# First slot of the expert projections: two token tiles per expert in turn, and all low halves of the weights on VectorE

## The chip, the cores and the metric

The kernel runs on one core of one Trainium2 chip. The metric is the device time of one execution in microseconds (us), as the median of several executions. The engines are TensorE (PE in the profile; PEld is its weight load), VectorE (DVE), ScalarE (ACT), GpSimd (POOL) and SyncE (SP), which issues most DMAs; ScalarE issues some too. Each engine works through its own list of instructions in order, and they meet through semaphores.

## What is computed

One block of a network on 4096 tokens of 256 channels: a normalised and modulated state space layer, and then an attention whose query, key, value and output projections are weighted sums over 16 experts. The part that matters here, cut from the reference:

```python
h = _layernorm(x) * (1 + ca) + sa
x = x + ga * attn_ref(h, ...)        # projection, short convolution, scan over tokens, gate, output projection
h = _layernorm(x) * (1 + cb) + sb
...
# n = 4096 tokens, c = 256, 16 experts, head size 128
logits = xn @ sn - sigmoid(gates)
w = softmax(masked relu(logits))     # at least two experts per token
def moe_proj(p):                     # p is q_proj, k_proj or v_proj: [16, 256, 128]
    y = einsum('nc,ech->neh', x, p)
    return einsum('ne,neh->nh', w, y)
q, k, v = moe_proj(q_proj), moe_proj(k_proj), moe_proj(v_proj)
attn = softmax(q k^T / sqrt(h))
out = sum over e of w[:, e] * (attn v) @ o_proj[e]
```

## The kernel before

The tokens are cut in 8 blocks of 512, each of 4 token tiles of 128. The first part of the kernel (to about 790 us) makes queries, keys and values, the second the attention. The first part is a row of 8 slots, one for each block: `slot(i, p, ahead)` for block 2i+p. A slot has 64 steps on TensorE, 4 tiles times 16 experts. **One step** is six matmuls (line 1793) that multiply one tile with one expert's query, key and value weights (384 columns) into one of four PSUM banks of `ps`: three for each half of the channels, since tokens and weights are kept as a high part and a low part (`xt_hi`, `xt_lo`, `w_hi`, `w_lo`). VectorE then adds the bank, times the token's weight for the expert, to `acc[:, t % 2]` (part of the memory `wst`; line 1478 for the first expert of a tile, line 1481 for the others), and counts `moe_acc`. TensorE may be three steps ahead of that (`wait(pe, moe_acc, ... s - MOE_BANKS + 1)`). Before, step s belongs to tile s // 16 and expert s % 16.

When a tile's 16 experts are summed, TensorE transposes its queries and keys into bank 7 (`qk_transposes`, lines 1698 and 1699), ScalarE rounds them and the values to high parts (`high_parts`, lines 842 and 845, counted by `v_hi_ready`), GpSimd makes the low part of the values (`low_v`, line 667, counted by `v_split`), VectorE that of queries and keys (`low_qk`, line 1264), and ScalarE issues the DMAs (`store_parts`). The first addition of tile t has to wait for `qk_mm` and `v_split` of tile t - 2, whose `acc` it writes over.

Between the steps stands the work of the next blocks, set by step numbers in a table (`DVE_PIECES`, `SCAN_AT`, `PE_Y`, ...). In the first slot they count from step 4 (`late`): r = s - 4. In the order of a slot these are, for block 1 (`c`): seven scan steps (TensorE line 1635, VectorE line 1112), `y_piece` at r = 24 (TensorE line 1652), the gate (VectorE line 1127), `out_piece` at r = 27 (TensorE line 1667), and `x2_piece` 0 at r = 29 (VectorE line 1140). For block 2 (`a`): `norm_piece` 0 to 4 on VectorE (lines 1023 and 1028, then 1039, 1046, 1023 and 1028, and 1033), in the first slot at the r of `LATE_NORMS`; `n2_transposes` at r = 20 (TensorE line 1563); `hidden` on ScalarE (lines 768 and 770 in turn), which counts `ht_ready`; and `project` from r = 31 (TensorE line 1579). Two waits matter. `y_piece` writes the banks that `hidden` reads and waits for it:

```python
if ahead >= 2 and not is_first(i, p):
    pe.wait_ge(ht_ready, upto(i, p, 1, 2))
```

And the first `project` of the slot waits for `x2_piece` 0, which reads those banks:

```python
if f == 0:
    pe.wait_ge(ht_lo_ready, upto(i, p, 1, 1))
    if i:
        pe.wait_ge(x2_ready, past(i, p, 1, 0, X2_MORE))
```

The low halves of the 16 experts' weights (`w_lo`) are made once, each by one subtraction of 128x768 elements. VectorE makes experts 0 to 7 ahead of the first slot and 8 to 10 in it (`split_w`, line 1018), GpSimd 11 to 15 (line 728), after `residual(0, 1)` (lines 628 and 632) and its part of `xt_lo` (line 723). In the first slot TensorE waits before each step of tile 0 for the expert's low half. VectorE makes the part of `xt_lo` that tile 0 needs (line 1456, `xlo_first`).

## Time and profile before

| what | us |
|---|---|
| median of 3 executions | 1403.19 |
| lowest and highest | 1401.58 and 1404.46 |
| the profiled execution | 1400.98 |
| its span | 1399.0 |
| TensorE busy in it | 1361.3 |
| VectorE, ScalarE, GpSimd busy in it | 1153.9, 685.4, 725.8 |

The span goes from the first to the last instruction of one execution. Some 2 us of the execution lie around it. Times of rows are counted from the span's start. The first slot's steps begin at 70.8 us. A row of an order of time has its start, its busy time, engine, line, operation, what is written and read, shapes and count; in brackets at its end stands how long the engine was idle before it and who ended that. A row can stand for several like instructions in a row, and its time is then from the first start to the last end.

### The profile page before, as it was taken

What the parts mean: (1) busy time and instruction counts of PE and PEld (TensorE: products, weight loads), DVE (VectorE), ACT (ScalarE), POOL (GpSimd) and SP (SyncE); (2) the same over time, 40 slices, a digit from 0 to 9 for tenths busy, and PEclk for the clock granted to TensorE, in tenths of its full rate; (3) what the DMA queues carried; (4) which work ended last, traced back from release to release, by engine and by line L of the source; (5) the groups of instructions that cost most, each with busy time, mean ns of one, the idle gap of its engine ahead of it and who ended that gap; (6) DMA issues with size and microseconds to landing.
All of it is one profiled execution on the core that took longest, in us unless ns stands there. A gap on an engine that the chain in (4) does not pass through costs nothing. (4 is left out here: it accounts for less than half of the span.)

```text
span 1399.0 us, 21090 instructions
## 1 busy us (share of the span) xinstructions
PE 1361.3 (97%) x6974; PEld 1204.5 (86%) x6974; DVE 1153.9 (82%) x2176; ACT 685.4 (49%) x1350; POOL 725.8 (52%) x641
## 2 busy tenths in 40 slices
PE   7989999999999999999999899999999999999997
PEld 5889999999999999999999777878787878788776
DVE  7886886868868778585778898989898989999866
ACT  4702314013121040320101598888888888888983
POOL 1551412214113140140123477888888888888897
PEclk9999999999999999999999999999999999999999
DMA  8201110111111101001147500000001010010000
GB/s 230 82 16 32 40 28 28 40 32 29 28 38 29 33 23 43 30 26 28 57 144 230 206 2 19 12 31 16 31 16 31 9 39 8 16 31 16 15 9 31
DMA packets 83389, 63.01 MB, mean 45 GB/s; under 512 B 14240, under 2 KB 76112, under 8 KB 83024
## 3 DMA queue, kind: packets, MB, share of 16 engines
q1 hardware_dynamic: 55136, 46.00, 10.5%
q10 hardware_dynamic: 28144, 15.67, 3.8%
q8 instruction: 55, 0.90, 0.3%
q14 instruction: 54, 0.44, 0.1%
HBM read 36.55 MB, written 25.03 MB: 44 GB/s over the span
## 5 line engine op out<-in xcount | busy, mean ns | idle before, releaser
L1793 PE MATMUL ps<-w_hi,memory_r 128*128 128x384 f32 x2048 | 561.2, 341 | 2.3 <-POOL w_lo L728 1.8
L1481 DVE SCALAR_TENSOR_TENSOR wst<-ps,w_cur,wst 128x384 f32<-128x384 f32 x480 | 295.2, 615 | 150.8 <-PE ps L1793 134.3
L2014 POOL TENSOR_TENSOR memory_rest<-memory_rest,pf 128x512 f32<-128x512 f32 x248 | 346.6, 1398 | 65.9 <-ACT pf L2121 57.2
L1793 PEld LDWEIGHTS ps<-w_hi,memory_r 128*128 128x128 f32 x2048 | 373.8, 188 | 6.9 <-issue 4.1
L1793 PE MATMUL ps<-w_lo,memory_r 128*128 128x384 f32 x1024 | 343.4, 335 | 0.0
L2187 DVE TENSOR_TENSOR p_lo<-pf,p_hi 128x512 fp32r<-128x512 f32 x256 | 281.8, 1101 | 33.1 <-ACT p_hi L2123 32.1
L1793 PEld LDWEIGHTS ps<-w_lo,memory_r 128*128 128x128 f32 x1024 | 192.6, 188 | 4.7 <-issue 1.4
L2121 ACT ACTIVATE pf<-ps 128x512 f32<-128x512 f32 x256 | 153.1, 598 | 72.3 <-PE ps L2293 54.3
L2081 ACT COPY ps<-shift_rows 128x512 f32<-128x512 f32 x254 | 151.7, 597 | 5.8
L2123 ACT ACTIVATE p_hi<-ps 128x512 fp32r<-128x512 f32 x256 | 152.0, 594 | 0.0
L2168 DVE TENSOR_REDUCE mx<-ps 128x1 f32<-128x512 f32 x224 | 147.7, 679 | 1.2 <-PE ps L2282 1.2
L667 POOL TENSOR_TENSOR wst<-wst 128x128 fp32r<-128x128 f32 x28 | 12.9, 461 | 239.8 <-ACT wst L845 239.8
L2204 DVE SCALAR_TENSOR_TENSOR memory_rest<-ps,w_out_s,memory_rest 128x256 f32<-128x256 f32 x252 | 120.7, 479 | 8.2 <-PE ps L2360 3.2
L1994 POOL TENSOR_TENSOR memory_rest<-memory_rest,act_half 128x256 f32<-128x256 f32 x112 | 108.1, 965 | 6.2 <-ACT act_half L2096 1.3
L2317 PE MATMUL ps<-p_hi,memory_kv 128*128 128x512 f32 x256 | 100.9, 394 | 7.4 <-DVE p_lo L2187 7.4
L2291 PE MATMUL ps<-memory_r 128*128 128x512 f32 x256 | 101.9, 398 | 5.5 <-ACT ps L2081 4.1
L842 ACT CAST wst<-ps 128x256 fp32r<-128x256 f32 x28 | 10.5, 373 | 194.5 <-PE ps L1699 194.1
L2360 PE MATMUL ps<-o_hi,ot_hi 128*128 128x512 f32 x256 | 100.0, 391 | 1.4 <-DVE ot_lo L2209 1.4
L2292 PE MATMUL ps<-memory_kv,memory_r 128*128 128x512 f32 x256 | 100.3, 392 | 0.0
L2293 PE MATMUL ps<-memory_r,memory_kv 128*128 128x512 f32 x256 | 100.3, 392 | 0.0
L2319 PE MATMUL ps<-p_lo,memory_kv 128*128 128x512 f32 x256 | 100.0, 391 | 0.0
L2318 PE MATMUL ps<-p_hi,v_lo 128*128 128x512 f32 x256 | 99.8, 390 | 0.0
(256 smaller groups left out, 2198.6 us busy)
## 6 DMA issues: line engine op xcount, KB each, us to landing
qk_scratch<-wst ACTq DMA_DIRECT2D x56, 128.0 KB, 2.2
x_scratch<-memory SPq DMA_DIRECT2D x8, 512.0 KB, 2.9
o_scratch<-memory_rest SPq DMA_DIRECT2D x16, 256.0 KB, 3.2
x2b<-x_scratch SPq DMA_DIRECT2D x32, 128.0 KB, 2.2
out_x<-memory_rest SPq DMA_DIRECT2D x32, 128.0 KB, 1.7
v_scratch<-wst ACTq DMA_DIRECT2D x60, 64.0 KB, 1.8
memory<-in_x SPq DMA_DIRECT2D x7, 512.0 KB, 4.1
memory_r<-qk_scratch SPq DMA_DIRECT2D x9, 256.0 KB, 4.4
```

Of the source, the lines that this page charges most:

```text
L1481: nc.vector.scalar_tensor_tensor(out=dst, in0=src, scalar=w, in1=dst, op0=ALU.mult, op1=ALU.add).then_inc(moe_acc, 1)
L1793: ins = nc.tensor.matmul(ps[:, s % MOE_BANKS, 0:H3], x_part[p][:, k, rows], w_part[:, k, e].rearrange("p t h -> p (t h)"), start=(k == 0 a ...
L1994: nc.gpsimd.tensor_tensor(total, total, halves[n], ALU.add).then_inc(act_summed, 1)
L2014: nc.gpsimd.tensor_tensor(p_sum[:, p], p_sum[:, p], pf[:, j % PB], ALU.add).then_inc(p_summed, 1)
L2081: nc.scalar.copy(ps[:, S_BANK + j % 2, :], shift_rows[:]).then_inc(seeded, 1)
L2121: nc.scalar.activation(pf[:, buf], ps[:, S_BANK + j % 2, :], ACT.Exp, scale=SCALE).then_inc(pf_ready, 1)
L2123: nc.scalar.activation(p_hi[:, buf], ps[:, S_BANK + j % 2, :], ACT.Exp, scale=SCALE).then_inc(p_hi_ready, 1)
L2168: nc.vector.tensor_reduce(mx[:, t, g:g + 1], ps[:, MAX_BANKS[j % 2], :], AX_X, ALU.max).then_inc(max_red, 1)
L2187: nc.vector.tensor_tensor(p_lo[:, j % PB], pf[:, j % PB], p_hi[:, j % PB].bitcast(F32), ALU.subtract).then_inc(p_lo_ready, 1)
L2204: nc.vector.scalar_tensor_tensor(out=y[:, t % 2], in0=src, scalar=w, in1=so_far, op0=ALU.mult, op1=ALU.add).then_inc(y_acc, 1)
L2291: nc.tensor.matmul(dst, k_hi[:, keys], q_hi[:, p], start=shifted, stop=False, skip_group_check=True)
L2317: nc.tensor.matmul(dst, v_hi[:, j], p_hi[:, buf], start=(j == 0), stop=False)
```

## The change

In the first slot alone, steps 0 to 31 take tiles 0 and 1 in turn for each expert: step s belongs to tile s % 2 and expert s // 2. VectorE makes the low halves of experts 0 to 5 ahead of the slot and those of 6 to 15 in it, one after each even step from step 6 to 24; GpSimd makes none. An addition then waits for the addition two steps back and not for the last one. Tile 0 is summed at step 30 and tile 1 at step 31, so the transposes of tile 0's queries and keys move from step 20 to step 33 and its `low_qk` from 22 to 35; tile 1's stay at 36 and 38. `LATE_NORMS` moves pieces 3 and 4 from r = 14 and 18 to 15 and 20, and `n2_transposes` moves from r = 20 to 23 in this slot; `y_piece` stays at r = 24. VectorE's first part of `xt_lo` grows from one tile to two. GpSimd's `residual(0, 1)` waits for the last `u_ready` of block 1 in place of the eighth low half. ScalarE and GpSimd take `hidden` and `low_hidden` of block 2 ahead of tile 0's parts.

```diff
-        LATE_SPLIT, POOL_SPLIT, SPLIT_AHEAD, FIRST_BU, FIRST_TAKE = 8, 11, 3, 3, 0
-        LATE_NORMS = {4: 0, 8: 1, 11: 2, 14: 3, 18: 4}
+        LATE_SPLIT, SPLIT_AHEAD, FIRST_BU, FIRST_TAKE, LATE_N2 = 6, 3, 3, 0, 3
+        LATE_NORMS = {4: 0, 8: 1, 11: 2, 15: 3, 20: 4}
...
+        def step(i, p, s):
+
+            if is_first(i, p) and s < 2 * E:
+                return s % 2, s // 2
+            return divmod(s, E)
+
+        def tile_sums(i, p, t):
+
+            return 2 * E - 1 + t if is_first(i, p) and t < 2 else (t + 1) * E
+
+        def tile_parts(i, p, s, at):
+
+            t, e = step(i, p, s)
+            if is_first(i, p) and s < 2 * E + at:
+                return 0 if s == 2 * E + at - 3 else None
+            return t - 1 if e == at and t else None
...
-                pool.wait_ge(w_lo_ready, LATE_SPLIT)
+                pool.wait_ge(u_ready, 2 * FI)
                 residual(0, 1)
-                rest = slice(P, BT)
+                rest = slice(2 * P, BT)
...
-                pool.wait_ge(w_lo_ready, POOL_SPLIT)
-                for n in range(POOL_SPLIT, E):
-                    pool.wait_ge(w_hi_ready, n + 1)
-                    nc.gpsimd.tensor_tensor(w_lo[:, :, n], w_raw[:, :, n], w_hi[:, :, n].bitcast(F32), ALU.subtract
-                                            ).then_inc(w_lo_ready, 1)
...
-                    if first:
-                        high(0)
                     if ahead >= 2:
                         hidden(*a)
-                    if not first:
-                        high(0)
+                    high(0)
                     store(0)
...
-                tt(xt_lo[0][:, :, 0:P], h2t[:, :, 0:P], xt_hi[0][:, :, 0:P].bitcast(F32), ALU.subtract
+                tt(xt_lo[0][:, :, 0:2 * P], h2t[:, :, 0:2 * P], xt_hi[0][:, :, 0:2 * P].bitcast(F32), ALU.subtract
...
-                split_w(6, LATE_SPLIT)
...
-                            dve.wait_ge(moe_acc, upto(i, p, STEPS, s))
+                            dve.wait_ge(moe_acc, upto(i, p, STEPS, s - 1 if is_first(i, p) and s < 2 * E else s))
...
-                        if is_first(i, p) and LATE_SPLIT <= s + SPLIT_AHEAD < POOL_SPLIT:
-                            split_w(s + SPLIT_AHEAD, s + SPLIT_AHEAD + 1)
+                        if is_first(i, p) and s % 2 == 0 and LATE_SPLIT <= s // 2 + SPLIT_AHEAD < E:
+                            split_w(s // 2 + SPLIT_AHEAD, s // 2 + SPLIT_AHEAD + 1)
...
-                            if r == PE_TRANSPOSE_N2:
+                            if r == PE_TRANSPOSE_N2 + (LATE_N2 if is_first(i, p) else 0):
                                 n2_transposes(*a)
```

TensorE from the transposes of block 2 (`ps<-ident,memory`) to `y_piece` (`ps<-st_parts,cm_parts`). Before, the transposes stand four steps of five rows each ahead of `y_piece`; these are the last step and `y_piece`:

```order
L1793 MATMUL ps<-w_hi,memory_r 128x384 [waits moe_acc]
L1793 MATMUL ps<-w_lo,memory_r 128x384
L1793 MATMUL ps<-w_hi,memory_r 128x384 x2
L1793 MATMUL ps<-w_lo,memory_r 128x384
L1793 MATMUL ps<-w_hi,memory_r 128x384
L1652 MATMUL ps<-st_parts,cm_parts 128x512 [waits ht_ready,st_in]
L1652 MATMUL ps<-st_parts,cm_parts 128x512 x2
```

The same place in the changed kernel (its line numbers are 11 to 15 higher there):

```order
L1574 MATMUL ps<-ident,memory 128x128 [waits n2_ready]
L1574 MATMUL ps<-ident,memory 128x128 x7
L1804 MATMUL ps<-w_hi,memory_r 128x384 [waits w_lo_ready,moe_acc]
L1804 MATMUL ps<-w_lo,memory_r 128x384
L1804 MATMUL ps<-w_hi,memory_r 128x384 x2
L1804 MATMUL ps<-w_lo,memory_r 128x384
L1804 MATMUL ps<-w_hi,memory_r 128x384
L1663 MATMUL ps<-st_parts,cm_parts 128x512 [waits ht_ready,st_in]
```

One step is left between the transposes and `y_piece`, where there were four.

ScalarE in the first slot, before: tile 0's parts (`wst<-ps`, `wst<-wst`), then `hidden` of block 2, then the stores:

```order
L842 CAST wst<-ps 128x256 [waits qk_mm]
L845 CAST wst<-wst 128x128
L768 ACTIVATE memory<-ps,lnb,lnw 128x512 [waits n2_transposed]
L770 ACTIVATE memory_r<-ps,lnb,lnw 128x512
L768 ACTIVATE memory<-ps,lnb,lnw 128x512
L770 ACTIVATE memory_r<-ps,lnb,lnw 128x512
L853 DMA qk_scratch<-wst 256x1x128 [waits qk_lo_ready,qk_ready]
```

And in the changed kernel:

```order
L783 ACTIVATE memory<-ps,lnb,lnw 128x512 [waits n2_transposed]
L785 ACTIVATE memory_r<-ps,lnb,lnw 128x512
L783 ACTIVATE memory<-ps,lnb,lnw 128x512
L785 ACTIVATE memory_r<-ps,lnb,lnw 128x512
L857 CAST wst<-ps 128x256 [waits qk_mm]
L860 CAST wst<-wst 128x128
L868 DMA qk_scratch<-wst 256x1x128 [waits qk_lo_ready,qk_ready]
```

`hidden` now comes first, and tile 0's parts stand directly ahead of its stores.

VectorE in the first slot, before, around the second part of the normalisation of block 2 (`memory<-memory,mv,modv`):

```order
L1481 SCALAR_TENSOR_TENSOR wst<-ps,w_cur,wst 128x384 [waits moe_acc,moe_mm] x2
L1112 TENSOR_TENSOR scan_b<-scan_b,ps 128x62 [waits scan_add,scan_mm]
L1481 SCALAR_TENSOR_TENSOR wst<-ps,w_cur,wst 128x384 [waits moe_acc,moe_mm] x2
L1112 TENSOR_TENSOR scan_b<-scan_b,ps 128x60 [waits scan_add,scan_mm]
L1039 SCALAR_TENSOR_TENSOR memory<-memory,mv,modv 128x256 [waits mv_ready,r_ready]
L1039 SCALAR_TENSOR_TENSOR memory<-memory,mv,modv 128x256 x3
```

And in the changed kernel:

```order
L1124 TENSOR_TENSOR scan_b<-scan_b,ps 128x62 [waits scan_add,scan_mm]
L1492 SCALAR_TENSOR_TENSOR wst<-ps,w_cur,wst 128x384 [waits moe_acc,moe_mm] x2
L1030 TENSOR_TENSOR w_lo<-w_raw,w_hi 128x2x384 [waits w_hi_ready]
L1124 TENSOR_TENSOR scan_b<-scan_b,ps 128x60 [waits scan_add,scan_mm]
L1051 SCALAR_TENSOR_TENSOR memory<-memory,mv,modv 128x256 [waits mv_ready,r_ready]
L1051 SCALAR_TENSOR_TENSOR memory<-memory,mv,modv 128x256 x3
L1492 SCALAR_TENSOR_TENSOR wst<-ps,w_cur,wst 128x384 [waits moe_acc,moe_mm] x2
L1030 TENSOR_TENSOR w_lo<-w_raw,w_hi 128x2x384 [waits w_hi_ready]
```

A low half stands after every second addition, ahead of the scan step that TensorE waits for.

## Rows read from the trace of the kernel before

**Rows 1.** The page's head, and the waits of TensorE, longest first, from 118 to 800 us

```profile
span 1399.0 us, 21090 instructions
...
PE ps L2291 <- ACT ps L2081: 1.4, 1, 1.4
```

**Rows 2.** Waits of TensorE from 70 to 135 us: us in total, times, longest

```profile
PE ps L1793 <- POOL w_lo L728: 1.8, 4, 0.5
PE ps L1635 <- DVE scan_b L1112: 1.3, 1, 1.3
PE ps L1563 <- DVE memory L1033: 1.1, 1, 1.1
```

**Rows 3.** TensorE in order of time, first slot

```profile
84.15 0.33 PE L1637 MATMUL ps<-scan_a,near 128*128 128x64 f32 x2
...
106.52 0.27 PE L1698 MATMUL ps<-ident,wst 128*128 128x128 f32 x1
...
112.16 1.09 PE L1563 MATMUL ps<-ident,memory 128*128 128x128 f32 x8 [1.06 <-DVE memory L1033]
113.00 0.42 PE L1793 MATMUL ps<-w_hi,memory_r 128*128 128x384 f32 x1
...
117.28 0.85 PE L1652 MATMUL ps<-st_parts,cm_parts 128*128 128x512 f32 x3
...
121.09 5.34 PE L1667 MATMUL ps<-wout,memory 128*128 128x256 f32 x24
126.08 0.52 PE L1793 MATMUL ps<-w_hi,memory_r 128*128 128x384 f32 x1
...
130.43 1.59 PE L1579 MATMUL ps<-memory_r 128*128 128x512 f32 x6
```

**Rows 4.** VectorE in order of time, from just ahead of the first slot

```profile
70.32 0.43 DVE L1456 TENSOR_TENSOR memory_r<-memory,memory_r 128x256 fp32r<-128x256 f32 x1 [0.51 <-ACT memory_r L985]
70.67 0.69 DVE L1377 TENSOR_TENSOR memory<-memory 128x512 f32<-128x512 f32 x1
...
81.11 2.77 DVE L1481 SCALAR_TENSOR_TENSOR wst<-ps,w_cur,wst 128x384 f32<-128x384 f32 x4
...
88.57 0.94 DVE L1018 TENSOR_TENSOR w_lo<-w_raw,w_hi 128x768 fp32r<-128x768 f32 x1
89.44 0.60 DVE L1481 SCALAR_TENSOR_TENSOR wst<-ps,w_cur,wst 128x384 f32<-128x384 f32 x1
89.96 0.20 DVE L1112 TENSOR_TENSOR scan_b<-scan_b,ps 128x63 f32<-128x63 f32 x1
90.09 1.39 DVE L1023 BATCH_NORM_STATS2 bst<-memory 128x6 f32<-128x256 f32 x4
...
91.93 1.31 DVE L1481 SCALAR_TENSOR_TENSOR wst<-ps,w_cur,wst 128x384 f32<-128x384 f32 x2
...
95.36 4.47 DVE L1039 SCALAR_TENSOR_TENSOR memory<-memory,mv,modv 128x256 f32<-128x256 f32 x4
...
101.75 1.66 DVE L1046 SCALAR_TENSOR_TENSOR memory<-memory,rs,modv 128x256 f32<-128x256 f32 x4
...
110.72 1.38 DVE L1033 TENSOR_SCALAR memory<-memory,mv,rs 128x256 f32<-128x256 f32 x4
...
129.08 1.21 DVE L1140 TENSOR_TENSOR memory<-memory,ps 128x1024 f32<-128x1024 f32 x1
```

**Rows 5.** GpSimd in order of time

```profile
89.59 9.17 POOL L728 TENSOR_TENSOR w_lo<-w_raw,w_hi 128x768 fp32r<-128x768 f32 x5 [2.42 <-DVE w_lo L1018]
...
138.89 0.46 POOL L667 TENSOR_TENSOR wst<-wst 128x128 fp32r<-128x128 f32 x1 [0.83 <-ACT wst L845]
```

**Rows 6.** ScalarE in order of time

```profile
106.94 0.37 ACT L842 CAST wst<-ps 128x256 fp32r<-128x256 f32 x1 [33.57 <-PE ps L1699]
...
115.29 0.78 ACT L770 ACTIVATE memory_r<-ps,lnb,lnw 128x512 fp32r<-128x512 f32 x1
...
138.24 0.37 ACT L842 CAST wst<-ps 128x256 fp32r<-128x256 f32 x1
```

More of the change, by code:

```diff
@@ L679, in split_o, with pieces @@
                                             ).then_inc(op_lo_ready, 1)
-                def pieces(ahead, c, a, tile):
+                def pieces(ahead, c, a, tile, first):
                     if ahead >= 2:
                         first_norms(*a)
-                    tile(0)
+                    if not first:
+                        tile(0)
                     if ahead >= 2:
                         low_hidden(*a)
+                    if first:
+                        tile(0)
                     second_norm(*c)
@@ L1470, in slot @@
                     for s in range(STEPS):
-                        t, e = divmod(s, E)
+                        t, e = step(i, p, s)
                         dve.wait_ge(moe_mm, upto(i, p, STEPS, s + 1))
@@ L1695, in qk_transposes @@
                 def qk_transposes(i, p, t):
-                    pe.wait_ge(moe_acc, upto(i, p, STEPS, (t + 1) * E))
+                    pe.wait_ge(moe_acc, upto(i, p, STEPS, tile_sums(i, p, t)))
                     wait(pe, qk_lo_ready, upto(i, p, TT, t))
@@ L1783, in slot @@
                     for s in range(STEPS):
-                        t, e = divmod(s, E)
+                        t, e = step(i, p, s)
                         wait(pe, moe_acc, upto(i, p, STEPS, s - MOE_BANKS + 1))
@@ L1787, in slot @@
                             pe.wait_ge(w_lo_ready, e + 1)
-                        if is_first(i, p) and s == E:
+                        if is_first(i, p) and s == 2 * E:
                             pe.wait_ge(xlo_ready, 1)
@@ L1799, in slot @@
                             qk_transposes(*before(i, p), TT - 1)
-                        if e == 4 and t:
-                            qk_transposes(i, p, t - 1)
+                        if tile_parts(i, p, s, 4) is not None:
+                            qk_transposes(i, p, tile_parts(i, p, s, 4))
                         if is_first(i, p) and s == FIRST_BU:
```

6 lines of the change are left out of this document (3 added, 3 removed).

## The prediction

> **What bounds the kernel now.** I read the page's head first and then the waits of TensorE. The page has TensorE busy for 1361.3 of 1399.0 us, and from 118 to 800 us its longest wait is 1.4 us [rows 1]. So what TensorE loses or gains up to the first projection of block 2, at 130.43 us, should stay to the end. The second look is at its waits from 70 to 135 us: 1.8 us for low halves that GpSimd makes, 1.3 us for the first scan addition, 1.1 us for the last part of a normalisation, `n2` [rows 2]. Together that is 4.2 us, and it is nearly all that a rearrangement of this slot can win. The third look is at the two lists in order of time, TensorE's and VectorE's [rows 3, 4]: the two waits that aren't for GpSimd are for VectorE results, and GpSimd's low halves hold up VectorE too, as will be seen. VectorE's list is what has to be added up.
>
> **Before the slot.** VectorE's piece of `xt_lo` stands between ScalarE's `xt_hi` and the first step. It took 0.43 us with 256 elements, and a subtraction or product of 512 took 0.69 [rows 4]. TensorE starts the slot 0.25 us later. The two low halves that leave VectorE's list here buy nothing: after step 3 TensorE does block 1's input term (24 matmuls), and VectorE's next copy waits for the last of them anyway; its additions start at 81.1 in either kernel, or 0.25 later [rows 4].
>
> **VectorE's list from step 8 to the `n2` piece.** Starts of neighbouring rows give prices [rows 4]: an addition with something else behind it 0.52 (89.44 to 89.96), a low half 0.87 (88.57 to 89.44), a scan addition 0.13 (89.96 to 90.09), a set of statistics 1.84 (90.09 to 91.93), a shift 1.66. The modulation took 4.47 us for four operations of the same form as the shift's, while GpSimd's five low halves ran from 89.59 to 98.76 [rows 5]; without them I take 1.66, a gain of 2.8 us. Two additions of one tile behind each other wait for each other: four took 2.77 us in all, so (2.77 - 0.62) / 3 = 0.72 from start to start. Two additions of different tiles behind each other stand nowhere in the trace. They cannot be cheaper than 0.52 and need not be dearer than 0.72; I take 0.52, because what follows an addition without needing its result starts after 0.52.
> The start: TensorE's first scan step stood at 84.15 [rows 3], now 84.4. Two steps of 1.04 (six matmuls) and the scan step's 0.36 later, with 0.2 for the way to VectorE, the addition of step 8 starts at 87.1. From there to the `n2` piece stand 17 additions (17 x 0.52 = 8.8), nine low halves (7.8), six scan additions (0.8), two sets of statistics (3.7), modulation and shift (3.3), and small copies (0.5, estimated from the 0.2 of a scan addition). That is 24.9 us: `n2` starts at 112.0 and ends 1.38 us later, at 113.4. TensorE's eight transposes start at 113.5 in place of 112.16.
> That is 1.3 us later, but three more steps (3.1 us) are done by then. At this point the change is ahead by 1.8 us. The list is the bound, and the five low halves that GpSimd no longer makes (5 x 0.87 = 4.4) eat more than the 2.8 us of the modulation; two additions by 0.2 us cheaper six times (1.2) pay for most of the rest.
>
> **A rule of the skill beside these prices.** The second of two additions started 0.72 us behind the first where it needed it, an independent operation 0.52 behind an addition of 0.60 [rows 4]. The Trainium skill ("VectorE: DVE Perf Modes", section "The DRAIN you can't avoid") says that the next VectorE operation does not start until the pipeline is empty and that a semaphore between two costs nothing extra. By that, additions in turn on two tiles would gain nothing and keep 0.72; the rows speak against it, but none of them has two such additions. It is a rival below.
>
> **`y_piece` takes the gain back.** It waits for ScalarE's `hidden`. Before, the transposes started at 112.16 and the last of `hidden`'s four activations ended at 115.29 + 0.78 = 116.07, 3.9 us behind [rows 3, 6]; the four steps between them hid that, and `y_piece` started at 117.28. Now one step is left. TensorE is there at 113.5 + 0.84 + 1.13 = 115.5, and `hidden` is done at 113.5 + 3.9 = 117.4. **A stall of 2.0 us** that before was none. `y_piece` starts at 117.5, 0.2 us later than before. Whatever VectorE's list gains or loses ahead of `n2` still goes through here one to one, because `hidden` follows the transposes.
>
> **The first projection gets a new wait.** From `y_piece` to `out_piece` TensorE took 3.81 us (117.28 to 121.09) and for `out_piece` 4.99 (to 126.08) [rows 3]. So step 32 starts at 126.3 and step 33 ends at 128.4. There stand tile 0's transposes, which were at 106.52, 20 us ahead of their user. VectorE's first addition of tile 2 (step 32) writes over tile 0's sums and now waits for this chain: transposes to ScalarE 0.42 (106.52 to 106.94), ScalarE to GpSimd 0.65 (138.24 to 138.89), GpSimd 0.46 [rows 3, 5, 6], and 0.05. It starts at 130.0 and not at 127.5. Behind it in VectorE's list stand the addition of step 33 (0.72) and `x2_piece` 0 (0.53 later, 1.21 long): its end is 132.4. Before, it was 129.08 + 1.21 = 130.29, and the projection started at 130.43 [rows 3, 4], just behind it. The projection now starts at 132.5, where TensorE would be ready at 130.7: **a stall of 1.8 us**, and 2.1 us later than before. The banks don't add to it, since step 36 is the first that needs the addition of step 32.
> What else is moved costs nothing. The store of tile 0, four DMA issues, now stands ahead of `data_out` in ScalarE's list, but TensorE needs the first result of that only for the fourth projection; the three ahead of it take 1.59 us each and have three steps of 1.04 between them, some 8 us [rows 3]. GpSimd's `residual` starts earlier, since it doesn't wait for low halves any more, and should be done with its three operations before VectorE's first low half of the slot; if not, that is part of rival 1. The load of block 2's input, SyncE's next DMA behind it, starts earlier with it. All of block 2's later work follows the same projections.
>
> **The sum.** +2.1 us at 130 us, carried to the end. The profiled execution took 1400.98, of which 1399.0 are its span; the changed one should show about 1401.1 in the span. The median was 1403.19, so I predict **1405.3 us**. 0.2% is 2.8 us, about what a measurement of this kernel can tell from no change; the forecast is inside it.
>
> **Rivals.**
> 1. *Additions in turn cost what they do in a row.* From step 8 to `n2` there are six pairs of additions with nothing between them. At 0.72 they cost 6 x 0.2 = 1.2 us more, `n2` is later by that, and it goes through `hidden` one to one: +3.3 us, **1406.5**. A collision of GpSimd's last piece with the first low half of the slot does the same; the modulation shows what such a collision can cost, 2.8 us over four operations [rows 4]. Beyond 0.7 us of such losses the kernel is slower by over 0.2%. Against it: the 0.52 of rows 4. Chance 0.2, and 0.1 for larger losses of this sort, about 1408.
> 2. *The wait of step 32 is hidden.* If `x2_piece` 0 isn't what the projection waits for, 0.3 us stay: **1403.5**. For it: before, the row of the projection shows no idle time. Against it: the two ends are only 0.14 us apart in the rows. Chance 0.15.
> 3. *The waits for low halves and scan go and little takes their place.* If VectorE were never late, TensorE would reach the transposes at 84.4 + 0.4 + 21 x 1.04 + 6 x 0.36, about 108.8, `y_piece` would follow at 112.7, 4.6 us early, and the wait at the projection would leave 2.6 us: **1400.6**; 1398.6 with that wait hidden as well. It needs 4.7 us out of VectorE's list, which the prices don't allow. Chance 0.1.
> 4. *The change hardly does anything*: VectorE's list comes out shorter by some 2 us and both stalls stay, 1403.2. Chance 0.05.
>
> **How the numbers follow.** The forecast has 0.4. Faster by over 0.2% is rival 3 and a little of what a median of few runs scatters (the three shown span 2.9 us): 0.11. Slower by over 0.2% is part of rival 1 (half of 0.2), the 0.1 of larger losses and a share of the forecast's own scatter: 0.29. Within it 0.6. The range reaches from the lower scatter of rivals 2 and 4, 1401.8, to 1408.0 for the larger losses.
>
> **What would show it.** In the changed trace: no wait of TensorE for a low half; GpSimd with no `w_lo`; the modulation at about 1.7 us; additions of tiles 0 and 1 at 0.52 from start to start; the transposes of block 2 near 113.5; an idle time of about 2 us ahead of `y_piece`, ended by ScalarE; idle time of VectorE ahead of the first addition of tile 2, ended by GpSimd; some 1.8 us of idle time ahead of the first projection, ended by VectorE's `x2`, near 132.5 us. The prediction is wrong if one of the two stalls is missing, or if TensorE gives back a part of the 2.1 us after 135 us.

## The result, and the profile after

| | before | changed |
|---|---|---|
| median of 20 executions each | 1402.10 us | 1404.74 us |
| lowest and highest | 1400.83 and 1404.47 | 1402.78 and 1407.84 |
| profiled execution, its span | 1400.98, 1399.0 | 1406.05, 1404.3 |

The ratio is 1.0019, with a 95% interval of 1.0013 to 1.0025: 2.6 us slower, where 2.1 were forecast. That is inside 0.2%, and the interval lies wholly above 1, so the loss is real.

The page's head after. TensorE does about the same work as before (1361.3 us), and GpSimd 11 us less (725.8):

```profile
span 1404.3 us, 21091 instructions
PE 1364.0 (97%) x6974; PEld 1207.9 (86%) x6974; DVE 1152.0 (82%) x2181; ACT 687.0 (49%) x1350; POOL 715.0 (51%) x636
```

TensorE's waits from 70 to 137 us after (columns as in [rows 2], whose lines these answer to). The low halves are gone from the list. The scan additions cost more than twice what they did, and two new lines stand where the prediction put them, 1.9 and 1.8 us:

```profile
PE ps L1646 <- DVE scan_b L1124: 2.8, 3, 1.0
PE ps L1663 <- ACT memory_r L785: 1.9, 1, 1.9
PE ps L1590 <- issue: 1.8, 1, 1.8
PE ps L1574 <- DVE memory L1045: 1.2, 1, 1.2
```

TensorE in order of time after; the last six rows answer to [rows 3]:

```profile
92.61 0.43 PE L1646 MATMUL ps<-scan_b,powers 128*128 128x60 f32 x2 [0.88 <-DVE scan_b L1124]
...
113.36 1.10 PE L1574 MATMUL ps<-ident,memory 128*128 128x128 f32 x8 [1.18 <-DVE memory L1045]
...
117.44 1.35 PE L1663 MATMUL ps<-st_parts,cm_parts 128*128 128x512 f32 x3 [1.93 <-ACT memory_r L785]
...
122.89 5.34 PE L1678 MATMUL ps<-wout,memory 128*128 128x256 f32 x24
...
130.15 0.27 PE L1709 MATMUL ps<-ident,wst 128*128 128x128 f32 x1
...
134.39 1.63 PE L1590 MATMUL ps<-memory_r 128*128 128x512 f32 x6 [1.76 <-issue]
```

The transposes of block 2 start at 113.36 (before 112.16), `y_piece` at 117.44 (117.28), `out_piece` at 122.89 (121.09) and the first projection at 134.39 (130.43). From `y_piece` to `out_piece` it took 5.45 us and not 3.81. The profile in stretches of 1 us says why (columns: stretch, its length, TensorE's busy time and matmuls, granted clock, DMA share, GB/s):

```profile
118.00:119.00 1.00, 1.00 (x4) 0.50 0.00 0
119.00:120.00 1.00, 1.00 (x5) 0.50 0.00 0
120.00:121.00 1.00, 1.00 (x5) 0.50 0.00 0
```

TensorE had been idle for 1.93 us up to 117.44, and from 118 to 121 us it ran at half of its clock (1.2 GHz in place of 2.4), with 0.87 and 0.93 in the microseconds on either side. That loss of 1.64 us was not in the prediction. It isn't in every execution, as a later run shows.

VectorE in order of time after, to be held against [rows 4]:

```profile
70.28 0.69 DVE L1468 TENSOR_TENSOR memory_r<-memory,memory_r 128x512 fp32r<-128x512 f32 x1 [0.51 <-ACT memory_r L997]
...
92.47 1.14 DVE L1492 SCALAR_TENSOR_TENSOR wst<-ps,w_cur,wst 128x384 f32<-128x384 f32 x2
93.52 0.95 DVE L1030 TENSOR_TENSOR w_lo<-w_raw,w_hi 128x768 fp32r<-128x768 f32 x1
...
94.51 1.67 DVE L1051 SCALAR_TENSOR_TENSOR memory<-memory,mv,modv 128x256 f32<-128x256 f32 x4
...
111.93 1.37 DVE L1045 TENSOR_SCALAR memory<-memory,mv,rs 128x256 f32<-128x256 f32 x4
...
131.82 0.62 DVE L1489 TENSOR_SCALAR wst<-ps,w_cur 128x384 f32<-128x384 f32 x1 [8.11 <-POOL wst L684]
...
133.07 1.21 DVE L1152 TENSOR_TENSOR memory<-memory,ps 128x1024 f32<-128x1024 f32 x1
```

Two additions of different tiles take 1.05 us from start to start of what follows (92.47 to 93.52), so 0.52 each. The modulation takes 1.67 (4.47 before). The `n2` piece starts at 111.93. VectorE then waits for GpSimd ahead of tile 2's first addition, and `x2_piece` 0 ends at 133.07 + 1.21 = 134.28, with the projection 0.11 behind it: that is what the 1.76 us called "issue" waited for.

**A zero for comparing traces.** Two profiled executions of like kernels can differ by 2 us in their first 17 us (last section). Positions below are therefore counted from one early instruction that no kernel here moves, the matmul `ps<-sim_sq,ones_f`. It starts at 47.10 in before and at 47.06 in the changed kernel, but at 49.19 in one of the others. "The new zero" is that instruction. The table's last column is the start of block 2's second set of transposes, `h2`, in the slot's second half; behind it all kernels do the same work.

| kernel, us from the new zero | `n2` transposes | `y_piece` | first projection | `h2` transposes |
|---|---|---|---|---|
| before | 65.06 | 70.18 | 83.33 | 101.35 |
| changed, first profile | 66.30 | 70.38 | 87.33 | 105.37 |
| changed, second profile | 66.34 | 70.40 | 85.81 | 103.87 |
| e1 (no projection stall) | 66.34 | 70.40 | 83.87 | 101.89 |
| e3 (neither stall) | 66.33 | 70.40 | 84.41 | 100.05 |
| e9 (e3, list shorter by two) | 65.21 | 69.22 | 83.21 | 98.85 |

(In e3 and e9 `y_piece` and the first projection stand two steps later in TensorE's list, so their starts aren't comparable with the rows above.)

### The profile page after: what moved, and what is told of

The parts are those of the page before. It is cut to its first block and busy times, and to the rows that moved or that the text cites. A ratio compares the mean times of both kernels' runs of the same rounds, so it can differ in the third digit from the quotient of the medians.

```text
span 1404.3 us, 21091 instructions
## 1 busy us (share of the span) xinstructions
PE 1364.0 (97%) x6974; PEld 1207.9 (86%) x6974; DVE 1152.0 (82%) x2181; ACT 687.0 (49%) x1350; POOL 715.0 (51%) x636
## 5 line engine op out<-in xcount | busy, mean ns | idle before, releaser
L2371 PE MATMUL ps<-o_lo,ot_hi 128*128 128x512 f32 x256 | 99.8, 390 | 0.0
```

The lines of the kernel that those rows point to most:

```text
L2371: ins = nc.tensor.matmul(dst, a[:, p, rows], b[:, 2 * pair:2 * pair + 2].rearrange("p e c -> p (e c)"), start=(n == 0), stop=(n == 2))
```

## The experiments

Each kernel was timed beside before on the same chip, most with 11 executions. The time of one kernel falls into two clusters some 2 us apart, and a median can jump between them; where under 1 us is discussed, I also give the difference of the means to before's of the same batch. Theory T is that of the prediction: the stall ahead of `y_piece` (2.0 us) and the wait ahead of the first projection (1.8 us) add up, and VectorE's list sets where the transposes stand. The changes are shown against the changed kernel unless it says otherwise.

### 1. The projection's stall alone

Tile 0's queries and keys are transposed right behind step 31, ahead of `out_piece`, and not at step 33.

```diff
-                return 0 if s == 2 * E + at - 3 else None
+                return 0 if s == (2 * E - 1 if at == 4 else 2 * E + at - 3) else None
```

> The changed kernel, but TensorE transposes tile 0's queries and keys behind step 31, ahead of out_piece, and not behind step 33. My theory: the first addition of tile 2 waits for the chain transposes, ScalarE, GpSimd, and x2_piece 0 and the first projection of block 2 behind it; with the transposes ahead of out_piece (5 us) the chain is hidden, so the idle time of 1.76 us of TensorE ahead of that projection goes, the projection starts some 1.7 us earlier, and the median is 1402.9 to 1403.2 (1404.7 for the changed kernel, 1402.1 before). Rival 2 of the prediction, by which the projection would be late for another reason: the idle time stays or turns into one at a later step, median 1404.7. Another rival: the transposes have to wait for the sum of tile 0 (step 30) there, which costs 0.5 us or more at step 31.

Measured: 1403.48 us against 1402.31 for before, ratio 1.0008 (0.9999 to 1.0017), mean +1.1; 0.3 us above the range expected. TensorE's waits from 70 to 140 us in this run:

```profile
PE ps L1646 <- DVE scan_b L1124: 2.8, 3, 1.0
PE ps L1663 <- ACT memory_r L785: 1.9, 1, 1.9
PE ps L1574 <- DVE memory L1045: 1.2, 1, 1.2
```

The wait ahead of the projection is gone and the other one unchanged. At the `h2` transposes it is 1.98 us ahead of the changed kernel's second profile (103.87 to 101.89), and the means give 1.8 (from +2.9 to +1.1 against before). So the term of 1.8 us is real, and the means show no part of it given back by the end.

### 2. The stall ahead of `y_piece` alone

`y_piece`, `out_piece`, `x2_piece` 0 and the projections stand two steps later, by a second table for this slot.

```diff
+        LATER = {30: ("gate", 0), 35: ("x2", 0), 37: ("x2", 1), 38: ("x2", 2), 39: ("x2", 3), 40: ("conv", 0),
+                 41: ("x2", 4), 43: ("conv", 1)}
+        def pe_place(i, p, s):
+            if is_first(i, p) and 28 <= s < 43:
+                return s - 6 if s >= 30 else -1
+            return s - late(i, p)
...
-                        r = s - late(i, p)
+                        r = pe_place(i, p, s)
```

> The changed kernel, but in the first slot y_piece, the gate, out_piece, x2_piece 0 and the projections come two steps later (y_piece behind step 30), so that three steps stand between the transposes of block 2 and y_piece. My theory: hidden (3.9 us from the start of the transposes) is then just covered and the stall of 1.9 us ahead of y_piece goes; median 1402.8. In the profiled execution of the changed kernel the granted clock was 0.5 from 118 to 121 us, right behind that stall, which made 1.6 us more; if the stall brought that on, the median is a little lower still, 1402.3 to 1402.8, and no stretch of the trace between 112 and 130 us is below 1.0. Rival: the stall only moves, because the later projections then wait (for ScalarE's copies or VectorE's convolution), median 1404 to 1405.

Measured: 1401.28 us, ratio 0.9992 (0.9984 to 1.0001), mean -1.0. It is faster than expected by more than 1 us, and the waits show that it took away more than one thing:

```profile
PE ps L1657 <- DVE scan_b L1133: 2.8, 3, 1.0
PE ps L1585 <- DVE memory L1054: 1.2, 1, 1.2
```

Both stalls are gone. With `out_piece` two steps later, tile 0's transposes at step 33 stand ahead of it, and ScalarE and GpSimd do their parts beside its 5 us. The run doesn't isolate the first stall. It shows that both have one cure.

### 3. Both edits together

> The two edits together: transposes of tile 0 ahead of out_piece, and y_piece and what follows it two steps later. My theory: the two stalls are behind each other on TensorE and independent, so their gains add up: 3.5 us below the changed kernel, median 1401.0 to 1401.4, which would be 0.7 to 1.1 us below the kernel before (1402.1). Rival: removing one lets VectorE's list be late at the next place (the projection), so that less than 2.5 us come: 1402.2 or more.

Measured: 1401.37 us, as expected, ratio 0.9991 (0.9982 to 1.0000), mean -0.9: the same as the second. From e1 to e3 the means differ by 2.0 and the `h2` transposes by 1.84 (101.89 to 100.05): that is the stall ahead of `y_piece`. So the two stalls were worth 1.8 and 2.0 us, and without them the change would have been about 0.9 us **faster** than before, not slower. The interval of the ratio just reaches 1; that e2 and e7 give the same (-1.0 and -0.9) speaks for a gain, and so does the `h2` column, 1.3 us ahead of before.

### 4. Tile 0's transposes behind `out_piece` again

If the chain over ScalarE and GpSimd is what `out_piece` hides in e2, then putting only the transposes behind it must bring the wait back. Against e2:

```diff
-                return 0 if s == 2 * E + at - 3 else None
+                return 0 if s == (2 * E + 2 if at == 4 else 2 * E + at - 3) else None
```

> The run with y_piece two steps later (e2), in which tile 0's transposes stand ahead of out_piece, since that moved behind them; here they are put one step behind out_piece (after step 34), so that the wait of VectorE at step 32 is back while y_piece's is not. My theory: the first addition of tile 2 starts 1.6 us after the transposes, four additions and tile 0's low part stand ahead of x2_piece 0, and TensorE loses 2.6 us up to the first projection: median 1403.9 (1401.3 without). If the early place of the transposes has no part in the 3.4 us that e2 gained on the changed kernel: 1401.3.

Measured: 1404.75 us, ratio 1.0014 (1.0005 to 1.0023), mean +1.9, so 2.9 above e2 where 2.6 were expected. TensorE's waits from 70 to 140 us have two new lines, 2.2 us together:

```profile
PE ps L1720 <- DVE wst L1285: 1.3, 1, 1.3
...
PE ps L1815 <- DVE wst L1498: 0.9, 1, 0.9
```

A step waits for VectorE's late first addition of tile 2 (line 1498), and tile 1's transposes wait for `low_qk` of tile 0, which reads bank 7 (line 1285). The `h2` transposes are 2.36 later than in e2. The mechanism holds; only where TensorE meets the late addition differs.

### 5. Rival 1: what do additions in turn cost?

Each addition waits for the last one again, and no other place changes.

```diff
-                            dve.wait_ge(moe_acc, upto(i, p, STEPS, s - 1 if is_first(i, p) and s < 2 * E else s))
+                            dve.wait_ge(moe_acc, upto(i, p, STEPS, s))
```

> The changed kernel, but every addition of the first 32 steps waits for the addition just before it and not for the one two steps back. This is rival 1 of the prediction made true. My theory: pairs of additions go from 0.53 to 0.72 us from start to start, six pairs between step 8 and n2 make 1.1 us, and the loss goes through hidden and y_piece one to one: the transposes start at 114.5 in place of 113.4, y_piece at 118.5, and the median is 1405.8. If the pace of the additions does not matter (TensorE is the bound there): 1404.7.

Measured: 1407.14 us (5 executions), ratio 1.0039 (1.0026 to 1.0051). VectorE in order of time in this run, and TensorE's transposes:

```profile
94.60 1.33 DVE L1492 SCALAR_TENSOR_TENSOR wst<-ps,w_cur,wst 128x384 f32<-128x384 f32 x2
```

```profile
116.49 1.09 PE L1574 MATMUL ps<-ident,memory 128*128 128x128 f32 x8 [1.56 <-DVE memory L1045]
```

A pair now takes 1.33 us, where it took 1.14. From the new zero (48.86 here) the transposes start at 67.63, 1.33 later than in the changed kernel; about 1.1 had been expected of six pairs at 0.2. So 0.2 us for each pair is what the additions in turn save, and rival 1 is out. The time missed its expectation (1405.8): it rose by more than the 1.3 us. The profile has a low clock in two places. One is right behind the idle time of 1.92 us ahead of `y_piece`, as in the changed kernel's first profile:

```profile
122.00:130.00 8.00, 8.00 (x36) 0.84 0.00 0
```

From 121 to 125 us it was 0.60, 0.50, 0.50 and 0.70. From `y_piece` to `out_piece` it took 5.49 us (120.55 to 126.04), again 1.6 more than in the changed kernel's second profile. The other place is 790 to 800 us, at 0.51. All five executions had a mean clock of 0.996 or below, where 9 of the changed kernel's 20 had. How much of the rest is that, five executions don't tell.

### 6. GpSimd's low halves alone

Before, with all remaining low halves on VectorE and none on GpSimd, in before's order of steps. Against before:

```diff
-        LATE_SPLIT, POOL_SPLIT, SPLIT_AHEAD, FIRST_BU, FIRST_TAKE = 8, 11, 3, 3, 0
+        LATE_SPLIT, POOL_SPLIT, SPLIT_AHEAD, FIRST_BU, FIRST_TAKE = 8, 16, 3, 3, 0
...
-                pool.wait_ge(w_lo_ready, POOL_SPLIT)
```

> The kernel before with one part of the change alone: VectorE makes the low halves of experts 11 to 15 in the first slot too (one after each of the additions of steps 8 to 12), GpSimd makes none; tiles in the old order. It tells what the turns of tiles 0 and 1 are worth. My theory: VectorE's list up to n2 gets five low halves (5 x 0.87 = 4.35 us) and loses 2.8 us at the modulation; with a new low half needed every step and two additions of one tile at 0.72, the transposes of block 2 start 1.5 us later than before, nothing else in the slot waits, median 1403.8 (1402.2 for the kernel before). Rival: low halves come so late, step by step, that TensorE loses 3 us or more: 1405 or more. Other rival: GpSimd's were what TensorE waited for (1.8 us of waits), and without them it is faster: 1400.5 to 1401.5.

Measured: 1402.32 us, ratio 0.9999 (0.9990 to 1.0008), mean -0.1. The waits:

```profile
PE ps L1634 <- DVE scan_b L1111: 1.9, 3, 1.3
PE ps L1792 <- DVE w_lo L1017: 1.8, 1, 1.8
```

The expectation had VectorE's list longer by 1.6 us (4.4 for the low halves less 2.8 for the modulation) and missed: the transposes moved by only 0.4. The rows of both traces give the rest. In before VectorE paused once in that list, 0.75 us ahead of the addition at 94.70, for a step that TensorE had started late; in this run it has no pause there. And four additions with low halves between them cost 0.52 each from start to start, where in before, partly in a row, they took 0.61: 0.4 us more. 4.4 - 2.8 - 0.75 - 0.4 is about the 0.4 measured. TensorE's 1.8 us in four waits became 1.8 us in one. Taking the work from GpSimd was neutral by itself, within the interval.

### 7. The transposes three steps earlier again

`LATE_N2` is 0 and the last `n2` piece stands behind step 22 again, as in before.

```diff
-        LATE_SPLIT, SPLIT_AHEAD, FIRST_BU, FIRST_TAKE, LATE_N2 = 6, 3, 3, 0, 3
-        LATE_NORMS = {4: 0, 8: 1, 11: 2, 15: 3, 20: 4}
+        LATE_SPLIT, SPLIT_AHEAD, FIRST_BU, FIRST_TAKE, LATE_N2 = 6, 3, 3, 0, 0
+        LATE_NORMS = {4: 0, 8: 1, 11: 2, 15: 3, 18: 4}
```

> The changed kernel with the last norm piece and the transposes of block 2 moved back to r = 18 and r = 20 (steps 22 and 24), all else as changed. My theory: four steps then cover hidden again and the stall ahead of y_piece goes, but TensorE is at step 24 early and waits longer for n2: the transposes start 1.9 us earlier than in the changed kernel with 2.4 us of idle time ahead, y_piece starts 0.9 us earlier than in the changed kernel, the stall of 1.8 us ahead of the projection stays. Median 0.9 us below the changed kernel, 1403.8. Rival: y_piece starts at the same time as in the changed kernel (hidden's chain is what counts, wherever it stands): 1404.7.

Measured: 1405.34 us, ratio 1.0019 (1.0010 to 1.0028), mean +2.6: no gain on the changed kernel, where 0.9 had been expected. The transposes' row (idle time at its end) and the stretch behind it:

```profile
113.82 1.09 PE L1574 MATMUL ps<-ident,memory 128*128 128x128 f32 x8 [2.71 <-DVE memory L1045]
```

```profile
112.00:118.00 6.00, 4.18 (x19) 0.74 0.02 4
```

The waits did nearly as expected: 2.71 us (2.4 expected) ahead of the transposes in place of 1.18, none ahead of `y_piece`, 1.73 ahead of the projection. The transposes start 1.93 us earlier (64.41 from the new zero), as expected. But in the profiled execution TensorE then ran at a mean of 0.74 of its clock from 112 to 118 us; in stretches of 1 us it is 0.50 from 115 to 118. That is (1 - 0.74) x 6 = 1.6 us at most, more than the gain: `y_piece` stands at 71.07, 0.7 later than in the changed kernel and not 0.9 earlier. The run leaves open whether that happens in every execution.

### 8. One low half earlier

e3, with low half 6 at step 3, where VectorE waits for TensorE's input term anyway, and one less behind the even steps. `FIRST_TAKE` also puts the additions of steps 1 to 3 ahead of the copy of that term. Cut from the edit:

```diff
-        LATE_SPLIT, SPLIT_AHEAD, FIRST_BU, FIRST_TAKE, LATE_N2 = 6, 3, 3, 0, 3
+        LATE_SPLIT, SPLIT_AHEAD, FIRST_BU, FIRST_TAKE, LATE_N2 = 7, 3, 3, 3, 3
...
+                        if is_first(i, p) and s == FIRST_TAKE:
+                            split_w(LATE_SPLIT - 1, LATE_SPLIT)
```

> The run with both stalls removed (e3), with a shorter list for VectorE: the additions of steps 1 to 3 and the low half of expert 6 stand ahead of the copy of block 1's scan input, in the 2.74 us in which VectorE waits for that input (after step 0). My theory: VectorE's list is what TensorE waits for between 84 and 114 us (2.8 us at scan steps, 1.2 us at the transposes); 2.4 us less of it bring the transposes of block 2 forward by 1.7 to 2.4 us, and that goes to the end: median 1399.0 to 1399.7, 0.2% below the kernel before. Rival: the waits at the scan steps are set by what stands just ahead of each scan addition in the list and not by its length; then less than 0.8 us come: 1400.6 or more.

Measured: 1401.71 us, ratio 0.9992 (0.9983 to 1.0001), mean -0.9, the same as e3. The transposes stand at 66.31 and did not move (expected 1.7 to 2.4 us earlier). The low half that left the list stood ahead of step 8's addition, and there VectorE waits for TensorE (0.38 us ahead of the row of the changed kernel at 87.08). Without that low half VectorE waits 0.74 and 0.42 us ahead of the additions of steps 7 and 8, and the latter starts where it did, 40.02 us from the new zero in both kernels. An operation taken out ahead of a pause only makes the pause longer.

### 9. Two low halves earlier, taken from the right end

e3, with low halves 6 and 7 at steps 3 and 4, and the other eight behind the even steps from 6 to 20; steps 22 and 24 have none.

```diff
-        LATE_SPLIT, SPLIT_AHEAD, FIRST_BU, FIRST_TAKE, LATE_N2 = 6, 3, 3, 0, 3
+        LATE_SPLIT, SPLIT_AHEAD, FIRST_BU, FIRST_TAKE, LATE_N2 = 8, 5, 3, 3, 3
...
+                        if is_first(i, p) and s in (FIRST_TAKE, FIRST_TAKE + 1):
+                            split_w(s - FIRST_TAKE + 6, s - FIRST_TAKE + 7)
-                        if is_first(i, p) and s % 2 == 0 and LATE_SPLIT <= s // 2 + SPLIT_AHEAD < E:
+                        if is_first(i, p) and s % 2 == 0 and s > 4 and LATE_SPLIT <= s // 2 + SPLIT_AHEAD < E:
```

> e7 shortened the wrong piece: it took the low half behind step 6 off VectorE's list, but VectorE waits for TensorE at step 8 anyway, and the nine low halves behind that stayed. Here two low halves (experts 6 and 7) and the additions of steps 1 to 3 stand in VectorE's idle time before step 5, and all others come one place earlier, behind steps 6 to 20, so that from step 8 to n2 stand seven and not nine. My theory, unchanged: TensorE's waits between 84 and 114 us (2.8 us at scan steps, 1.2 us ahead of the transposes) are the length of VectorE's list from step 8 on; two low halves less (1.7 us) bring the transposes of block 2 forward by 1.7 us against e3 and e7, and the median to 1.7 us below e3: some 2.6 us below the kernel before. Rival: only what stands directly ahead of a scan addition counts; then the transposes come less than 0.8 us earlier.

Measured: **1400.79 us against 1402.53 for before, ratio 0.9986 (0.9977 to 0.9995)**, mean -2.0. It beats both kernels, by little, but clear of the interval. TensorE's waits are down to one line, and the transposes no longer wait:

```profile
PE ps L1659 <- DVE scan_b L1133: 2.7, 3, 1.0
```

```profile
114.37 1.03 PE L1587 MATMUL ps<-ident,memory 128*128 128x128 f32 x8
```

The gain on e3 is 1.1 us of the means, where 1.7 were expected, and 1.1 to 1.2 in the positions (66.33 to 65.21 and 100.05 to 98.85). It is the wait of 1.2 us ahead of the transposes. VectorE's `n2` piece starts 1.45 us earlier than in the changed kernel (63.42 from the new zero, 64.87 there), and from there TensorE's own steps set the time. The missing 0.3 to the 1.7 is at the front: the two low halves taken earlier cost 1.31 and 1.52 us from start to start beside GpSimd's work, where 0.87 is usual, and the addition of step 8 starts 0.27 later. The scan waits didn't move (2.7 us). My reading is that each is made by what stands directly ahead of that scan addition in VectorE's list, as here ahead of the one at 100.49; no run moves a low half away from there alone:

```profile
98.47 1.14 DVE L1501 SCALAR_TENSOR_TENSOR wst<-ps,w_cur,wst 128x384 f32<-128x384 f32 x2
99.53 0.94 DVE L1039 TENSOR_TENSOR w_lo<-w_raw,w_hi 128x768 fp32r<-128x768 f32 x1
100.39 0.18 DVE L1256 COPY w_all<-w_cur 128x64 f32<-128x64 f32 x1
100.49 0.20 DVE L1133 TENSOR_TENSOR scan_b<-scan_b,ps 128x56 f32<-128x56 f32 x1
```

### 10 and 11. Is it the idle time that brings the low clock?

The changed kernel, with TensorE busy ahead of `y_piece` on products of constants that nobody reads; and the changed kernel once more, unaltered, on the same chip.

```diff
+                                if is_first(i, p):
+                                    fill(QK_BANK, 16)
```

> The changed kernel with 16 empty matmuls of 128 columns (1.8 us) on TensorE just ahead of y_piece, in its idle time of 1.9 us; they write a bank that nobody reads. It tells whether the idle time brings on the stretch at half clock that the profiled execution of the changed kernel shows right behind it (118 to 121 us, 1.6 us lost). My theory: y_piece and all that follows it keep their times, no stretch between 112 and 126 us is below 1.0, and the median and mean are 0.3 to 0.8 us below those of the changed kernel on the same chip, since fewer executions have a mean clock of 0.996 or less. Rival: the stretch comes from elsewhere: as many executions with a low clock as the changed kernel, same time. Other rival: the fills delay y_piece, 0.2 us or more slower.

> The changed kernel once more, on the same chip as the two runs beside it, as what they are compared with. My theory: 2.1 us of stalls on the path to the first projection, and in a part of the executions 1.6 us more from half clock behind the stall ahead of y_piece: median 2.3 to 2.9 us above the kernel before on this chip. The two stalls (1.9 and 1.8 us) stand in the trace with the same lengths; whether the half clock does is open.

Measured: 1405.60 us (mean 1405.30) with the filling, where 0.3 to 0.8 less than without had been expected, and 1405.65 (mean 1405.30) without, just above the range expected; the ratios to before are 1.0020 (1.0011 to 1.0030) and 1.0021 (1.0013 to 1.0030). The filling was too long, which spoils the trial. I had counted 16 products of 0.11 us; the trace has 32 records:

```profile
115.30 3.73 PE L1740 MATMUL ps<-ident 128*128 128x128 f32 x32
```

`y_piece` is 1.4 us later for that (71.78 from the new zero, 70.40 without) and so is everything up to the attention's first matmul (740.59 and 739.13), and yet the times are equal. Only 1 of the 9 executions with the filling had a mean clock of 0.996 or below, and 9 of the 11 without. In the two profiled executions the difference doesn't lie in the slot, where both show a full clock, but at the boundary of the two parts of the kernel. The filled kernel, and then the plain one:

```profile
780.00:790.00 10.00, 7.58 (x37) 0.92 0.13 36
790.00:800.00 10.00, 8.61 (x33) 0.91 1.10 349
```

```profile
780.00:790.00 10.00, 7.58 (x30) 0.76 0.28 81
790.00:800.00 10.00, 8.61 (x30) 0.73 1.10 377
```

The plain kernel's second profile is of worth for another reason. Its stalls have the same lengths as in the first (1.89 and 1.74 us), but the granted clock behind the first is full:

```profile
112.00:118.00 6.00, 2.92 (x18) 1.00 0.00 0
118.00:122.00 4.00, 4.00 (x24) 1.00 0.00 0
```

So the half clock at 118 to 121 us comes in some executions only. Without it, the changed kernel is 2.5 us behind before at the first projection (85.81 to 83.33) and at the `h2` transposes (103.87 to 101.35), which is near the difference of the medians, 2.6 and 3.1 in the two batches.

## Why the prediction was right, point by point

**VectorE's list to `n2`.** Forecast start 112.0, measured 111.93; transposes forecast at 113.5, measured 113.36. The start of the slot was as told (the part of `xt_lo` takes 0.69), the modulation too (1.66 and 1.67), and so was the price of additions in turn (0.52), which experiment 5 confirms from the other side. One comparison in that reasoning was wrong, and did no harm. The prediction credited the removal of GpSimd's low halves with 2.8 us in VectorE's list and charged 4.4 for taking them over; experiment 6 shows that against before the exchange moves the transposes by 0.4, since before had a pause and dearer additions there. The sum of the changed kernel's list was still right, because it was built from its own rows and not from that difference.

**The rule beside the prices.** Additions waiting for the one just before started 0.72 us apart (e4), those waiting for the one two back 0.52 (the changed kernel), at a busy time of 0.61 to 0.62 in both. The Trainium skill ("VectorE: DVE Perf Modes", section "The DRAIN you can't avoid") has a semaphore between two operations cost nothing extra. For this form of operation the runs disagree: 0.2 us for each wait on the operation just before.

**The stall ahead of `y_piece`.** Forecast 2.0 us and a start at 117.5; measured 1.93 and 117.44, and 1.9 in each profile that has it. e1 and e3 price it at 2.0.

**From `y_piece` to `out_piece`.** Forecast 3.81 us, as before; measured 3.92 in the second profile and 5.45 in the first. The half clock behind the idle time was in no term and in no rival. It is a part of why the profiled execution's span is 5.3 us longer than before's when the medians differ by 2.6: 2.35 us are there at the attention's first matmul without it (second profile), 1.5 are the half clock, and 1.5 come behind that matmul (below). The two profiled executions also lie at opposite ends of their kernels' scatter (before 1.1 us below its median, the changed one 1.3 above).

**The wait ahead of the projection.** Forecast 1.8 us, measured 1.76 and 1.74; e1 takes it away alone and e8 brings the chain back. From tile 0's transposes to the projection it took 4.24 us (130.15 to 134.39), and the forecast's terms gave 4.1. The way there was longer than told: from `out_piece` to the projection 11.49 us in the second profile (121.30 to 132.79), where the forecast had 11.2. That 0.3 and the 0.1 of the item above are most of the distance from +2.1 to the +2.5 measured at the projection. So the mechanism held at each step, and these two terms were a little too small.

**Carried to the end.** From the `h2` transposes to the attention's first matmul before took 635.43 us (101.35 to 736.78 from the new zero) and the changed kernel 635.27 and 635.26. Nothing is given back up to there. Behind it something is lost on top, which the prediction had at nothing. From the attention's first matmul to the end of the span before took 615.12 us and the changed kernel 616.60 and 616.39, and TensorE's granted clock from 780 to 800 us was 1.00 in before, 0.84 and 0.65 (per 10 us) in the changed kernel's first profile, 0.76 and 0.73 in its second. The stalls are not what this needs: e3, e7 and e5, which have neither, took 616.37, 616.22 and 616.23 at 0.66 to 0.82, while e1, e6 and e10, which have one of them, took 614.97, 614.83 and 614.80. So +2.35 us, at the attention's first matmul of the second profile, are the stalls and the small terms above; the rest up to the medians' +2.6 and +3.1 (means +2.9 and +3.0) is explained only in part. The forecast of +2.1 is a ratio of 1.0015, inside the measured interval.

**The rivals.** Rival 1 fell with the 0.52 us of the changed kernel's own rows, and e4 shows its price; rival 2 fell with the 1.76 us that the projection waits. Rival 3 (faster) needed the transposes at 108.8; they came at 113.36, and VectorE is late by its waits (2.8 and 1.2 us), as the prices said. Rival 4 needed a shorter list. The half clock is a rival that was not on the list.

**Where the gain of the change is.** From 23.4 us behind the new zero, at the slot's start, to the `h2` transposes before takes 77.95 us, with TensorE busy for 73.10 of them, and e3 takes 76.64, with 72.40. The low halves' waits of 1.8 us and one of 0.5 for an addition went, the scan's grew by 1.5: of the 1.3 us gained 0.6 are idle time, and the other 0.7 are busy time of the same work, which no run explains. The stalls, 3.8 us, turned the gain into a loss.

**Where the median stood.** The forecast was made on a median of 3, 1403.19; over 20 executions before's is 1402.10. With that as a base the forecast would have been 1404.2, and the measured median is 1404.74. That the forecast's own figure, 1405.3, is only 0.6 off is partly luck: its base was 1.1 too high and its difference 0.5 too small.

## What to carry to other kernels

When an operation is moved closer to its consumer, count the latency of what lies between them on the *other* engines: here two chains, one of 3.9 us over ScalarE and one of 4.1 us over ScalarE, GpSimd and VectorE, lost the steps or the matmul group that had covered them, and that decided the sign. A list of instructions on the engine that sets the pace has to be added up between its pauses: taking an operation out ahead of a pause gains nothing (e7), and taking it out behind the last pause gains up to the length of the wait at the list's end (e9: 1.1 of 1.7 us). For the scan additions in the middle of the list the order just ahead of each seems to matter and not the list's length, which was not tried by itself.

## What the runs showed of the hardware that was not expected

**Half clock behind short stalls, sometimes.** Behind an idle time of TensorE of 1.9 us ahead of `y_piece` the granted clock was 0.50 for about 3 us in two profiles (the changed kernel's first, 1.93 us, and e4, 1.92) and full in two others (e1, 1.92, and the changed kernel's second, 1.89); behind 2.71 us it was 0.50 for about 3 us in the one profile of e6. Ahead of each stall of 1.9 us the engine had waited another 1.2 to 1.6 us for `n2`. Behind the 1.7 to 1.8 us ahead of the projection, where the engine had been busy before, it was full in all five profiles that have that wait. None of the profiles without a stall of 1.9 us or more has a low clock in the slot, e10 among them. This fits the idle time as the cause, but it is single profiles. How much of the changed kernel's loss is the clock, over all its executions, isn't settled. The 11 of its first 20 executions with a mean clock of 0.997 or more average 1404.19 us and the other 9 average 1406.17, against 1402.20 for all 20 of before (in the later batches four of before's executions in five have 0.997 or more). So with a nearly full clock the changed kernel is about 2 us slower, which is what was forecast.

**A low clock at the boundary of the two parts.** e10 spends 1.4 us more on filling and is no slower; its profile regains that behind 780 us and not in the slot. Over all profiles the time from the attention's first matmul to the end is 614.8 to 615.1 us in before, e1, e2, e6 and e10, and 616.2 to 616.6 in the changed kernel, e3, e4, e5, e7 and e8, with e9 between at 615.9. From 780 to 800 us the granted clock is 0.74 to 0.76 on average in the second group, e8 apart (0.92), and 0.91 to 1.00 in the first and in e9. Why it differs between kernels that differ only 650 us earlier stays open, and it limits what a difference of 1 us in the medians says about the slot.

**Two clusters of times from the first 17 us.** The modulation's matmuls, which wait for the weights `wmod`, in before and in e2:

```profile
11.08 3.70 PE L1534 MATMUL ps<-memory 128*128 128x512 f32 x8 [0.73 <-DMA memory<-in_wmod]
```

```profile
10.99 5.88 PE L1556 MATMUL ps<-memory 128*128 128x512 f32 x8 [0.78 <-DMA memory<-in_wmod]
```

Eight matmuls take 3.70 us in one and 5.88 in the other, and the matmul taken above as zero stands at 47.10 and 48.92. The wait for the DMA is the same (0.73 and 0.78 us); it is the matmuls that are slower, a median of 1.04 us each in place of 0.59, and their weight loads, 0.34 in place of 0.19. The six profiles with a late zero (e2, e3, e4, e6, e7, e9) all have a median of 0.88 to 1.06 us there, and the seven with an early zero one of 0.59. Matmuls ahead of them, at 6.5 us, are alike in before and e2. The times look like the two levels of the clock, but the granted clock reads 1.00 in both, so the cause isn't shown. No kernel's edits touch this place. It is as large as what was studied here, so spans should be compared from a point behind it.

**A product of 128x128 float32 values takes two records of 0.11 us**, 0.22 together (32 records in 3.5 us for 16 products, e10).
